# Subtracting the softmax maxima inside the query–key contraction, and summing four of sixteen scan products unfolded on TensorE

## Time and profile before

| | |
|---|---|
| median of 3 runs | 830.47 us (830.2 to 832.67) |
| profiled execution, its own time | 829.18 us |
| its span in the profile | 827.4 us, mean granted PE clock 0.933 |
| busy, share of the span | PE 83%, PEld 58%, DVE 83%, ACT 63%, POOL 75% |
| scans (L1720) | 128, 292.3 us, first at 28.4 us, last ends at 600.4 us |
| folds on POOL (L1513) | 128, 161.3 us |
| identity sums on PE (Y<-prod,ident) | 512 instructions, 141.3 us |

### The profile page before, as it was taken

How to read it: one execution, slowest core, us unless ns; L and a number is a source line. 1 busy time by engine, 2 the same in 40 slices (tenths; PEclk the granted TensorE clock), 3 DMA queues, 4 the chain that set the end, 5 groups by cost and what they waited for, 6 DMA issues and landing times. The chain is left out here.

```text
span 827.4 us, 12371 instructions
## 1 busy us (share of the span) xinstructions
PE 685.5 (83%) x3923; PEld 477.2 (58%) x3923; DVE 683.8 (83%) x1041; ACT 522.6 (63%) x1223; POOL 619.2 (75%) x467
## 2 busy tenths in 40 slices
PE   6578759897898888889898798874778899899991
PEld 3453426555565555556555455552557678899981
DVE  3679999999999999999999999999953555865673
ACT  4687847787966977796697789567124334333353
POOL 1359988878899999999999999899752254675542
PEclk9679678999999999999999999989799999999997
DMA  4536595454538646534734644376064344886773
GB/s 106 205 116 163 183 280 183 127 202 161 156 125 225 211 152 199 169 130 128 228 136 154 190 158 154 109 237 211 27 211 127 97 139 128 268 294 219 230 257 102
DMA packets 80411, 142.70 MB, mean 172 GB/s; under 512 B 10555, under 2 KB 53574, under 8 KB 80346
## 3 DMA queue, kind: packets, MB, share of 16 engines
q1 hardware_dynamic: 75802, 133.38, 51.5%
q0 software_dynamic: 4544, 8.54, 2.9%
HBM read 110.25 MB, written 37.27 MB: 178 GB/s over the span
## 5 line engine op out<-in xcount | busy, mean ns | idle before, releaser
L1508 POOL TENSOR_TENSOR prod<-hst,BC 128x1024 f32<-128x1024 f32 x128 | 301.0, 2360 | 48.6 <-DVE hst L1720 40.0
L1720 DVE TENSOR_TENSOR_SCAN hst<-dA,Rp 128x1024 f32<-128x1024 f32 x128 | 292.3, 2284 | 9.0 <-ACT dA L1203 0.4
L1203 ACT ACTIVATE dA<-dtm,Aneg 128x255 f32<-128x255 f32 x512 | 213.9, 495 | 52.6 <-DVE hst L1720 52.0
L1513 POOL TENSOR_TENSOR prod<-prod 128x512 f32<-128x512 f32 x128 | 161.3, 1270 | 2.4
L1711 DVE TENSOR_TENSOR Rp<-BC,Rp 128x1024 f32<-128x1024 f32 x128 | 156.9, 1226 | 6.0 <-DMA BC<-bcd 0.6
L1628 POOL DMA_INDIRECT y2d<-prod,back x78 | 77.2, 990 | 101.6 <-DVE prod L2091 85.4
L649 PE MATMUL Y<-prod,ident 128*128 128x256 f32 x512 | 141.3, 409 | 14.3 <-POOL prod L1513 12.2
L649 PEld LDWEIGHTS Y<-prod,ident 128*128 128x128 f32 x512 | 101.4, 206 | 52.1 <-issue 19.1
L649 PE MATMUL Mb<-hpad,winT 128*128 128x512 f32 (+1 forms) x176 | 79.6, 598 | 14.5 <-ACT xh L1152 11.9
L649 PEld LDWEIGHTS Rp<-BC,xh 128*128 128x128 f32 x624 | 75.3, 192 | 7.7 <-ACT xh L1449 4.1
L649 PE MATMUL Rp<-BC,xh 128*128 128x128 f32 x624 | 76.4, 276 | 3.5 <-ACT xh L1449 3.5
(11 more groups left out here) (282 smaller groups left out, 1127.0 us busy)
## 6 DMA issues: line engine op xcount, KB each, us to landing
BC<-bcd SPq DMA_DIRECT2D x63, 1024.0 KB, 5.4
BC<-recs SPq DMA_DIRECT2D x39, 578.0 KB, 4.2
xsd<-blank SPq DMA_DIRECT2D x17, 1056.0 KB, 11.9
dtm<-xsd SPq DMA_DIRECT2D x39, 132.0 KB, 4.1
recs<-in_L_ffn_W SPq DMA_DIRECT2D x16, 256.0 KB
xin<-in_x SPq DMA_DIRECT2D x8, 256.0 KB, 5.2
x2d<-x2o SPq DMA_DIRECT2D x8, 256.0 KB, 5.6
E<-x2d SPq DMA_DIRECT2D x4, 512.0 KB, 6.8
```

The source lines that it names most:

```text
L1203: m = A(dA[:, k % RING, i, 1:SEQ], dtm[:, r % 2, d, b * SEQ + 1:(b + 1) * SEQ], ACT.Exp, scale=Aneg[:, d, c * NC + i:c * NC + i + 1])
L1508: TT(prod[:, k % RING, :, :], hst[:, k % RING, :, :], BC[:, (k // 2) % BCR, 1, :, :], ALU.mult).then_inc(s_pd, 1)
L1513: TT(prod[:, k % RING, 0:NC // 2, :], prod[:, k % RING, 0:NC // 2, :], prod[:, k % RING, NC // 2:NC, :], ALU.add).then_inc(s_fd, 1)
L1720: v.tensor_tensor_scan(hst[:, k % RING].rearrange("p n s -> p (n s)"), dA[:, k % RING].rearrange("p n s -> p (n s)"), U.rearrange("p n s - ...
```

## The change

The maxima are put, negated by a factor in the keys, into the contraction itself. `qT` has rows that are zero; the maxima, in float32, are copied there, and `Kbd` gets -1 in those rows. So the product of queries and keys comes out with the maximum subtracted.

- Gone: `split_max` with its five DVE operations and the wait on it before the U of step 14; the four `selmax` matmuls in each group of `scores_t`. The eight mask matmuls of a group become four bf16 ones of 64 rows x 256.
- `turn_max` makes four float32 transposes of 128x128; `copy_max` makes four copies of 32x512 in place of one of 96x512.
- `Kbd` is held twice (w = 0, 1), so `key_blocks` has eight activations, each with a bias and a scale per partition, in place of four with a scale.
- In steps 2, 5, 10 and 13 of each round POOL leaves out the fold, and PE sums all four products (eight instructions in place of four).
- Once, in round 0: six more small DVE operations for the constants, two transposes and one copy for the mask; one constant fewer is loaded.

```diff
+        WHOLE = 2, 5, 10, 13
+        def folded(r, k):
+            return r * (STEPS - len(WHOLE)) + sum(f not in WHOLE for f in range(k + 1))
 (sum_states)
-                pe.wait_ge(s_fd, r * STEPS + k + 1)
-                for i in range(NC // 2):
+                if k in WHOLE:
+                    pe.wait_ge(s_pd, r * STEPS + k + 1)
+                else:
+                    pe.wait_ge(s_fd, folded(r, k))
+                parts = NC if k in WHOLE else NC // 2
+                for i in range(parts):
 (scores)
-                        mm(T[h][:, w * SEQ:(w + 1) * SEQ], qT[rows, w, b, t * P:(t + 1) * P], Kbd[rows, b, :, :],
+                        mm(T[h][:, w * SEQ:(w + 1) * SEQ], qT[rows, 1 - w, b, t * P:(t + 1) * P], Kbd[rows, 1 - w, b, :, :],
 (turn_max)
-                pe.wait_ge(Tv.sem, Tv.at("me", r))
+                pe.wait_ge(Tv.sem, Tv.at("mx3b", r))
-                    m = pe.transpose(Tb[0:96, i * P:(i + 1) * P], nm[:, i, :, :], identb[:, :])
+                    m = pe.transpose(T[0][:, i * P:(i + 1) * P], mx[:, i, :], ident[:, :])
 (scores_t)
-                        o, hp = T[h][:, i * SEQ:(i + 1) * SEQ], TRIO[g][h][i]
-                        mm(o, selmax[:, hp, :], nmT[:, b * SEQ:(b + 1) * SEQ], start=False, stop=False, skip_group_check=True)
-                        for t in range(QT):
-                            m = mm(o[:, t * P:(t + 1) * P], mbias2[:, t, :, :], identb[:, :], start=False, stop=True,
+                        rows = slice(64 * h, 64 * h + 64)
+                        m = mm(T[h][:, i * SEQ:(i + 1) * SEQ], twice[rows, :, :], mbiasT[rows, :], start=False, stop=True,
 (key_blocks)
-                for j in range(HP // 2):
-                    m = A(Kbd[:, :, j, :], KT[:, :, :], ACT.Copy, scale=blk4[:, j:j + 1])
+                for w in range(2):
+                    for j in range(HP // 2):
+                        m = A(Kbd[:, w, :, j, :], KT[:, :, :], ACT.Identity, bias=kshift[:, w, j:j + 1], scale=kscale[:, w, j:j + 1])
 (copy_max)
-                A(nmT[:, :], Tb[0:96, 0:NB * SEQ], ACT.Copy).then_inc(Ta.sem, 1)
+                for w in range(2):
+                    for h in range(2):
+                        rows = slice(64 * h + 32 * (1 - w), 64 * h + 32 * (2 - w))
+                        m = A(qT[rows, w, :, :].rearrange("p b s -> p (b s)"), T[0][rows, :], ACT.Copy)
+                m.then_inc(Ta.sem, 1)
 (POOL body)
                 for f in folds[k]:
-                    fold(r, f)
+                    if f not in WHOLE:
+                        fold(r, f)
 (DVE inputs)
-                if r and k == 14:
-                    v.wait_ge(Tv.sem, Tv.at("me", r - 1))
 (DVE slot, step 13)
                         maxima(r - 1, 3)
-                        split_max(r - 1)
```

More of the change, by code:

```diff
@@ L100, in decoder @@
         mean = sb("mean", [P, P])
-        selmax = sb("selmax", [96, HP, P], BF16)
-        pickmax = sb("pickmax", [96, HEADS])
+        twice = sb("twice", [P, 2, KEYS], BF16)
         blk = sb("blk", [P, HEADS])
@@ L325, in decoder @@
         Ta = Marks(sem("Ta"), "KT V sq ln rs q m e00 e01 e10 e11 ld rd x2")
-        Tv = Marks(sem("Tv"), "xq " + " ".join(f"mx{i}a mx{i}b" for i in range(NB * QT)) + " ma mb mc md me n")
+        Tv = Marks(sem("Tv"), "xq " + " ".join(f"mx{i}a mx{i}b" for i in range(NB * QT)) + " n")
         s_kb = sem("s_kb")
+        s_mk = sem("s_mk")
         s_cT = sem("s_cT")
@@ L803, in scores_t @@
                         rows = slice(64 * h, 64 * h + 64)
[L804 removed]
+                        mm(T[h][:, i * SEQ:(i + 1) * SEQ], Kbd[rows, i, b, 2 * g:2 * g + 2, :], qT[rows, i, b, :],
                            start=i == 0, stop=False, skip_group_check=True)
@@ L994, in _, with turn_mask @@
             mm(T[0][:, SEQ:SEQ + 1], attT[:, 3, :], bv[:, :]).then_inc(s_tr, 1)
+            def turn_mask():
+                pe.wait_ge(s_k, 3)
+                pe.wait_ge(s_cT, 2)
+                for t in range(QT):
+                    m = pe.transpose(Tb[:, t * P:(t + 1) * P], mbias2[:, t, :, :], identb[:, :])
+                m.then_inc(s_mk, 1)
             def first_round(k):
@@ L1218, in copy_contexts, with copy_mask @@
                 A(cT[:, 4 * n:4 * n + 4, :], T[n][:, :].rearrange("p (r k) -> p r k", r=4), ACT.Copy).then_inc(s_cT, 1)
+            def copy_mask():
+                act.wait_ge(s_mk, 1)
+                A(mbiasT[:, :], Tb[:, 0:SEQ], ACT.Copy).then_inc(s_mk, 1)
             def twice_contexts(r):
@@ L1736, in maxima @@
                     v.wait_ge(Tp.sem, Tp.at(f"s{i}{'ab'[h]}", r))
[L1737 to L1752, removed]
+                    to = mx[:, i, 64 * h:64 * h + 64].rearrange("p (u x) -> p u x", u=2)[:, :, 0:HP // 2]
+                    v.tensor_reduce(to, T[h][:, :].rearrange("p (u j k) -> p u j k", u=2, k=KEYS), AX.X, ALU.max).then_inc(Tv.sem, 1)
             def normalise(r):
@@ L1923, in _ @@
             nxt_(v.tensor_copy(identb[:, :], ident[:, :]))
-            nxt_(v.tensor_copy(selmax[:, :, :].rearrange("p g (h k) -> p (g h) k", h=2), pickmax[:, :].unsqueeze(2).to_broadcast([96, HEADS, KEYS])))
+            for h in range(2):
+                half = slice(64 * h, 64 * h + 64)
+                nxt_(v.tensor_copy(twice[half, :, :], ident[half, half].unsqueeze(1).to_broadcast([64, 2, KEYS])))
             v.wait_ge(s_prea, 1)
@@ L1942, in attention_scale @@
                 nxt_(v.tensor_reduce(quads[:, :], blk[:, :].rearrange("p (q j) -> p q j", j=HP // 2), AX.X, ALU.add))
-                nxt_(v.tensor_tensor(qscale[:, :], quads[:, 0:2], quads[:, 2:4], ALU.add))
-                nxt_(v.tensor_scalar(qscale[:, :], qscale[:, :], float(HD) ** -0.5, None, ALU.mult))
+                nxt_(v.tensor_tensor(parity[:, :], quads[:, 0:2], quads[:, 2:4], ALU.add))
+                nxt_(v.tensor_scalar(qscale[:, :], parity[:, :], float(HD) ** -0.5, None, ALU.mult))
                 nxt_(v.tensor_scalar(qbias[:, :], qscale[:, :], bq[:, 0:1], None, ALU.mult))
+                for w in range(2):
+                    o = (1 - w) * GW
+                    nxt_(v.tensor_scalar(kscale[:, w, :], blk4[:, :], parity[:, w:w + 1], None, ALU.mult))
+                    nxt_(v.tensor_tensor(kshift[:, w, :], ident[:, o:o + HP // 2], ident[:, 64 + o:64 + o + HP // 2], ALU.add))
+                    nxt_(v.tensor_scalar(kshift[:, w, :], kshift[:, w, :], -1.0, None, ALU.mult))
             def routing_constants(k):
```

30 lines of the change are left out of this document (16 added, 14 removed).

## The result

Four runs of the changed kernel gave a median of **863.0 us** (860.7 to 866.3), beside 830.3 for the kernel before on the same chip: a ratio of 1.039, 95% interval 1.036 to 1.041. So it is slower, at the two places that the forecast named, and by 32.7 us where 19.5 were forecast; 863.0 lies 4 us above the range.

What follows compares the result with a forecast made beforehand. DVE's full list was taken to set each round, if its inputs come in time. Place 1's + 8.9, place 2's + 11.8 and the tail's + 0.3 gave + 21.0 on 829.2 us; forecast 850, range 836 to 859.

Steps and rivals of the forecast that it cites:

- place 2: End of step 9, where DVE's att_normed takes ACT's L1117: margin 0, later by 2.0 us in six rounds, + 11.8.
- place 1: End of step 15, where DVE takes ACT's copy for steps_x: margin 0.16 us, rounds 1 to 6 together + 8.9.
- rival (a): ACT's 15 free us per round cover its extra work, so DVE keeps the split's 1.3 us: 820 us; chance 0.12.
- part 1: split_max leaves DVE's list: 1.30 us in rounds 1 to 7, 9.1 us, only if steps_x is ready earlier too.
- part 2: Way from maxima to ACT's copy for step 15: sum + 0.3, transposes + 0.25, copies + 1.5, together 2.05 us later.
- part 3: key_blocks ahead of step 9's att_normed: eight activations at 0.42 us, + 2.0 in each of six rounds, + 11.8.
- Rival (c): TensorE's clock drops after longer idle gaps, 0.5 to 1 us more per round: 855 to 859 us; chance 0.08.
- part 4: POOL loses 5 us of folds per round, PE gets about + 1.5: worth nothing, unless POOL was about to bind.
- part 5: One-time work in round 0, six small DVE operations: 0 to + 1.4 us, taken as 0.
- part 6: Tail: last steps of round 7 - 1.0, key_blocks + 2.0, last attention's turn_max and groups - 0.7; + 0.3 us.

Runs made afterwards that it cites:

- the kernel with the early copy: Changed kernel with ACT's copy for step 15 put ahead of the decays, the first exps and the second half of inverse_roots_x: 838.5 us, ratio 1.008.
- both edits: Keys spread by GpSimd and ACT's copy for step 15 taken early: 823.1 us in the changed kernel, 838.4 us in the kernel before.

## Why the prediction was right or wrong

Of the 15.8 us by which the profiled executions differ more than the forecast, 4.6 are at place 2, 2.8 at place 1, 3.3 in the tail, 3.3 at the start and 1.8 in the rest. The first two are the prediction's own terms, and the experiments show their causes.

**Right: what bounds, and where it would break.** DVE sets the round, the busy shares do not say whether its inputs come in time, and the two waits of ACT appeared at exactly the places with margins of 0.16 and 0 us. With both taken away (823.1 us) the rest comes out near the 820 that rival (a) gave for a kernel in which ACT takes it all in; that rival fell only because ACT did not.

**Right: part 1.** The split's 1.3 us are lost while `steps_x` is late, and come back when it is not (rounds of 69.8 for 71.2).

**Right, with one size off: part 2.** The unfolded sum (+ 0.30, and 0.3 in the run without it) and the transposes (+ 0.22 for 0.25) were priced rightly. The step "I take the plain copy, the nearest row", 0.50 us, was not: copies of 32x512 stand 0.60 apart, + 1.91 for + 1.5. That is 0.4 in each of six rounds, 2.4 of the 2.8 by which place 1 is above its + 8.9. In round 6 it is the difference between the 0.6 to 0.7 of wait that the forecast's - 0.6 amounts to and the 1.03 that came. The bound of 1.2 to 2.3 held. Fewer partitions indeed give nothing back.

The rate in the Trainium skill, ScalarE: Activation LUTs, Rules for kernel authors, gives as an estimate 2.9 us for the four copies; 2.41 were measured, nearer to the rows' 2.0 than to that. For the eight key activations the same estimate is 3.2 to 3.3, and 3.20 were measured; its 1.6 for the added ones is below the 1.91 only because the four of the kernel before, with a scale alone, took 1.29.

**Right in its own size: part 3.** 0.40 us for an activation of 128x128 with bias and scale, + 1.91 for + 2.0, and a wait of 1.80 at full clock.

**Wrong: what the way through PE costs.** The step that failed is "in it ACT is busy or waits for PE matmuls ..., so nothing absorbs it": true, but it took those matmuls' time as fixed. At place 2 the low clock was 16.4 - 6 x 1.8 = 5.6 us over six rounds in the changed kernel, in rounded parts 1.3, 1.4, 0.6 and 1.4 in rounds 2, 4, 5 and 6 through the gate matmuls, 0.4 in each of rounds 3, 4 and 5 through the wait ahead of `KT`, and 0.2 less in round 1 for its margin. Rival (c), at 0.08, named the mechanism. Its 0.5 to 1 us a round holds as a mean (0.9), and its 855 to 859 is passed because the copies' 2.8 and the tail's 3.3 stand beside it.

TensorE is not slower over all: by the granted clock it spent 40 us of rounds 1 to 6 at the low clock before and 43 after. Before, these stretches lay mostly 48 us behind a round's first scan, where nobody waits for PE; after, at 15 and 35 us. After the first of these ACT waits for PE ahead of `KT`, and the second lies under the gate matmuls. The same total at a worse place. The total does not set the time: the two runs with eight key activations beside the changed kernel spent 63 us each at the low clock and took 859.2 and 849.9. What puts a stretch where it is stays open. An idle time of 2.49 us was followed by one in round 4 of the changed kernel and not in round 3, and one of 3.23 in round 3 of the kernel with the early copy and not in round 6.

**Right: part 4.** In the kernel before the unfolding is worth nothing. POOL's waits grew by 57 us from 98 to 600 us, 28.2 for the scan and 51.2 for PE's sums against 15.0 and 7.6: 8 a round and a little more, as forecast, but most of them with PE as releaser. The clause "unless POOL was about to bind" got its case in the kernel without unfolding and with the keys on POOL.

**Right: part 5.** Round 0 is 0.9 us longer, inside its 0 to + 1.4, and 1.7 shorter (74.1 for 75.8) in the change without its unfolding. **The start** is 3.3 us longer: sixteen of the first matmuls, instruction for instruction the same, took 6.75 us for 3.72. A low clock is not shown for them: the granted clock reads 1.00 in both profiles from 14 to 24 us, where they run. It reads 0.83 there in three other kernels, whose first scan is at 30.2 to 30.4 us. Why they were slow stays open. Kernels with the same start as the changed one have their first scan at 28.3 (keys on POOL) to 31.8 us, and kernels with the start of the one before at 28.4 to 30.4, so the change by itself does not make it.

**Wrong: part 6.** Tail + 3.6 for + 0.3. Of it 2.8 are there when the first expert tile is ready, 18.1 us after the last scan, not 15.3. In the first 25 us of the tail the granted clock was 0.81, and 1.00 in the kernel before. In the other kernels with the change that first tile is ready 18.1 us behind the last scan at 0.81 (keys on POOL), 16.6 at 0.88 (both edits), 16.5 at 0.89 (no unfolding), 15.3 at 0.94 and 15.2 at 0.93 (the copy early, without and with the unfolding, the first with the keys on POOL). With the copy taken early, the tail takes 227.7 us, 0.7 more than before. So the sum of part 6 stands, and the clock is the likely rest; the lower it is in these runs the later the tile, nearly in order, but it was not tried by itself.

## What to carry to other kernels

Where the bounding engine is full, read the margin at each place where it takes something from another engine, and price what is put ahead of that place on the other engine; the other's free time elsewhere in the round says nothing. Where the way runs through TensorE after it has idled, price its matmuls at both clock levels. And before a change that makes such a way longer is dropped, move the waited-for instruction ahead, and the new work to the engine that the change has freed: here two such edits turned + 4% into - 1%, and a part that had been worth nothing by itself, the unfolding, became worth 11.7 us.

## What the runs showed of the hardware that was not expected

- ACT's copies of 32x512 from PSUM start 0.60 us apart, while the 96x512 copy to bf16 was followed after 0.50 by an activation that writes another tile. Neither the output tile nor the type makes the 0.10: in the kernel before, a copy of 128x512 float32 from PSUM (L1218) was followed after 0.48, and two `exps` of 128x512 float32 that write one tile start 0.49 apart. The copies with fewer partitions were the longer ones here; why is open.
- POOL multiplies and adds per partition (two scalars, 128x128) in 0.45 us on average, eight in 3.45 us, and only multiplies (one scalar, kernel before with both edits) in 0.61: the operation with more in it was the shorter one. These are two kernels and two operand forms; the cause is open.
- The same four gate matmuls, 0.50 us each at 2.4 GHz, took 1.98, 2.46, 3.36 or 3.53 us in four places, after idle times of 2.19 or 3.24, 3.35, 2.49 and 3.23.
